# A graph and expert layer on one core: the first rows of x read and normalised ahead of the preparation of the edges

## What is computed

```python
edge_index = jnp.stack([src, dst])
xn = _layernorm(x, axis=-1)
x = x + _L0_gnn_ref(xn, edge_index, ...) + _L0_mix_ref(xn[None], w_qkv, w_proj, b_proj)[0]
x = x + _L0_ffn_ref(_layernorm(x, axis=-1)[None], ...)[0]
```

## Time and profile before

| | us |
|---|---|
| median of 3 runs | 1607.23 |
| lowest and highest | 1606.2, 1609.92 |
| the profiled execution | 1605.74 |
| its span in the trace | 1603.9 |
| mean granted clock of PE | 0.989 |

### The profile page before, as it was taken

One profiled execution on the slowest core, in us unless ns is written; L12 is line 12 of the kernel. 1 busy time (PEld: TensorE's weight loads), 2 busy tenths in 40 slices (PEclk: granted clock), 3 DMA queues, 4 the chain that ended last, 5 costly groups with the idle time before them and its releaser, 6 DMA issues.

```text
span 1603.9 us, 22049 instructions
## 1 busy us (share of the span) xinstructions
PE 1536.1 (96%) x8432; PEld 1025.1 (64%) x8433; DVE 791.6 (49%) x1503; ACT 347.0 (22%) x525; POOL 369.9 (23%) x422
## 2 busy tenths in 40 slices
PE   5999999999999899999989999999999999999996
PEld 3566676568889899999886555444444444444442
DVE  8655557886668799876987143111111111111111
ACT  3321122112240445640671110100000100000000
POOL 1187855653300000000000047011111111111111
PEclk9999999999999999999899999999999999999998
DMA  9900010000034427114203248834538211613450
GB/s 259 362 2 2 2 62 1 1 1 1 1 81 118 120 56 210 37 20 106 59 1 103 105 113 178 281 117 154 208 103 283 91 49 49 216 45 120 147 202 21
DMA packets 85339, 163.81 MB, mean 102 GB/s; under 512 B 18874, under 2 KB 48816, under 8 KB 85001
## 3 DMA queue, kind: packets, MB, share of 16 engines
q1 hardware_dynamic: 66903, 119.07, 23.4%
q0 software_dynamic: 12096, 23.27, 6.3%
q10 hardware_dynamic: 6258, 20.40, 4.6%
HBM read 127.75 MB, written 37.56 MB: 103 GB/s over the span
## 4 chain that ended last, share of the span: by engine, by line
PE 83%; DVE 9%; issue 2%; DMA 2%; ACT 1%; SPq 0%; DVEq 0%; POOL 0%; ACTq 0%; POOLq 0%
PE bank L816 33%; PE bank L1651 7%; PE bank L1689 6%; PE bank L1553 5%; PE bank L1466 5%; PE bank L1610 5%; PE bank L1438 4%; PE bank L726 2%; DVE arena L2419 2%; PE bank L1491 2%; PE bank L736 2%; PE bank L754 2%; DVE arena L2388 2%; PE bank L1737 1%; PE bank L810 1%
## 5 line engine op out<-in xcount | busy, mean ns | idle before, releaser
L816 PE MATMUL bank<-arena 128*64 128x384 f32 x3312 | 541.3, 488 | 0.6 <-ACT arena L890 0.6
L816 PEld LDWEIGHTS bank<-arena 128*64 128x64 f32 x3312 | 237.4, 137 | 292.8 <-issue 292.0
L1178 DVE SCALAR_TENSOR_TENSOR arena<-bank,arena 64x384 f32<-64x384 f32 x88 | 50.3, 610 | 356.2 <-DMA arena<-out_dram,arena 209.0
L1689 PE MATMUL bank<-arena 125*125 125x198 f32 (+1 forms) x1200 | 192.4, 322 | 10.3 <-DVE arena L2388 10.1
L1689 PEld LDWEIGHTS bank<-arena 125*125 125x125 f32 x1200 | 186.3, 196 | 14.4 <-DVE arena L2388 14.2
L1651 PE MATMUL bank<-arena 128*125 128x192 f32 x960 | 163.5, 328 | 1.1 <-DVE arena L2341 1.1
L1651 PEld LDWEIGHTS bank<-arena 128*125 128x125 f32 x960 | 157.7, 189 | 1.4 <-DVE arena L2341 1.4
L1344 POOL TENSOR_SCALAR arena<-arena 128x125 bf16<-128x125 f16 x186 | 115.3, 622 | 111.4 <-PE bank L1491 107.0
L2228 DVE TENSOR_TENSOR arena<-arena,bank 125x417 f32 x186 | 109.8, 590 | 52.4 <-PE bank L1491 43.3
L1338 POOL DMA_INDIRECT slot_table<-arena x80 | 112.0, 1400 | 93.4 <-issue 93.4
L707 POOL DMA_INDIRECT out_dram<-arena x44 | 40.1, 912 | 296.1 <-DVE arena L1178 296.1
(11 more groups left out here) (307 smaller groups left out, 1591.7 us busy)
## 6 DMA issues: line engine op xcount, KB each, us to landing
arena<-in_L_ffn_w_gate_dram SPq DMA_DIRECT2D x9, 2304.0 KB, 9.1
arena<-in_L_ffn_w_up_dram SPq DMA_DIRECT2D x9, 2304.0 KB, 10.8
arena<-in_L_ffn_w_down_dram SPq DMA_DIRECT2D x9, 2304.0 KB, 9.2
arena<-score_rows ACTq DMA_DIRECT2D x18, 585.9 KB
expert_in<-arena SPq DMA_DIRECT2D x23, 384.0 KB, 10.5
arena<-expert_in ACTq DMA_DIRECT2D x23, 384.0 KB, 3.5
arena<-in_L_mix_w_qkv_dram SPq DMA_DIRECT2D x2, 2304.0 KB, 17.6
xn_columns<-arena SPq DMA_DIRECT2D x1, 3750.0 KB, 14.8
```

The source lines that it names most:

```text
L816: ins = tp.matmul(ps[bank][HP * h:HP * h + HP, 0:384], frm[:, b, k, HP * h:HP * h + HP], ew[h][i][:, k, n * 384:(n + 1) * 384], start=(k = ...
L1689: ins = tp.matmul(ps[bank][0:T, c * width:(c + 1) * width], ptile[0:T, j % NPT, dt * T:(dt + 1) * T], values(n - first, st), start=(st == ...
```

## The change

Instructions are moved, one is added and one table load goes away. On SP, the two DMAs of rows 0 are issued ahead of the two DMAs of the edges. On DVE, the preparation of the edges is cut into `edges_as_float` (one cast) and `edge_places` (eleven instructions); the statistics of rows 0 come first, then the cast, then `normalise_rows(0)`, then the places. The one-hots and the key features are dealt out anew behind that. On PE, the transpose of the columns is now `turn_columns`, behind `turn_x(0)` and `turn_x(1)`. On ACT, a square root of one constant column is written to a scratch element as soon as the constants are ready, and the copy of the columns is now `take_columns`, behind `take_x(1)`.

```diff
--- before.py
+++ after.py
@@ -1208,8 +1208,6 @@
 
         @block.sync
         def _(sp):
-            sp.dma_start(ei[0:T, 0:EC], src.rearrange("(p c) -> p c", p=T)).then_inc(s_edges, 16)
-            sp.dma_start(ei[0:T, EC:2 * EC], dst.rearrange("(p c) -> p c", p=T)).then_inc(s_edges, 16)
             def rows_in(g):
                 rows_dma(sp, xs[0:T, 2 * g:2 * g + 2], x_rows[:, 2 * g:2 * g + 2], s_x[g])
 
@@ -1218,6 +1216,8 @@
                              w_qkv[:, D + hf * 384:D + (hf + 1) * 384].rearrange("(k p) n -> p k n", p=P)).then_inc(done, 16)
 
             rows_in(0)
+            sp.dma_start(ei[0:T, 0:EC], src.rearrange("(p c) -> p c", p=T)).then_inc(s_edges, 16)
+            sp.dma_start(ei[0:T, EC:2 * EC], dst.rearrange("(p c) -> p c", p=T)).then_inc(s_edges, 16)
             key_weights(0, s_wb[0])
             rows_in(1)
             key_weights(1, s_wk1)
@@ -1353,8 +1353,11 @@
         def _(pe):
 
             pe.wait_ge(s_const, 9)
-            pe.wait_ge(s_cin, 96)
-            tp.transpose(ps[7][:, 0:38], rowsin[0:38, :], ident[0:38, 0:38]).then_inc(s_colps, 1)
+
+            def turn_columns():
+                pe.wait_ge(s_cin, 96)
+                tp.transpose(ps[7][:, 0:38], rowsin[0:38, :], ident[0:38, 0:38]).then_inc(s_colps, 1)
+
             def turn_x(t):
 
                 pe.wait_ge(s_xn, t + 1)
@@ -1441,6 +1444,7 @@
 
             turn_x(0)
             turn_x(1)
+            turn_columns()
             key_product(0, 0)
             key_product(1, 0)
             turn_x(2)
@@ -1765,8 +1769,12 @@
             act.dma_start(rowsin[28:36, 0:C2], a_dst1.rearrange("h (f p) -> (h f) p", p=C2)).then_inc(s_cin, 16)
             act.dma_start(rowsin[36:38, 0:C2], b2.rearrange("(k p) -> k p", p=C2)).then_inc(s_cin, 16)
             act.wait_ge(s_const, 9)
-            act.wait_ge(s_colps, 1)
-            sc.activation(cols, ps[7][:, 0:38], ACT.Copy).then_inc(s_cols, 1)
+            sc.activation(junk8[0:T, 0:1], epst[0:T], ACT.Sqrt)
+
+            def take_columns():
+                act.wait_ge(s_colps, 1)
+                sc.activation(cols, ps[7][:, 0:38], ACT.Copy).then_inc(s_cols, 1)
+
             def ln_std(n):
                 lo, hi = LN_GROUPS[n]
                 act.wait_ge(s_stats, n + 1)
@@ -1790,6 +1798,7 @@
             ln_std(0)
             take_x(0)
             take_x(1)
+            take_columns()
             ln_std(1)
             key_exp(0, 0)
             key_exp(1, 0)
@@ -1977,29 +1986,32 @@
             stt = dv.scalar_tensor_tensor
 
 
-            dve.wait_ge(s_edges, 32)
-            step(dv.tensor_copy(ef[0:T], ei[0:T]))
...
-            dve.wait_ge(s_const, 9)
+            def edges_as_float():
+                dve.wait_ge(s_edges, 32)
+                step(dv.tensor_copy(ef[0:T], ei[0:T]))
+
+            def edge_places():
+                step.wait()
+                step(dv.tensor_scalar(pi[0:T], ef[0:T], 6554.0, None, ALU.mult))
+                step.wait()
...
+                dve.wait_ge(s_const, 9)
 
 
             def half(row, i):
@@ -2141,21 +2153,23 @@
                 stt(out=kbuf[t % 4][0:T, hf * 384:(hf + 1) * 384], in0=kexp[0:T, i % 2], scalar=1.0,
                     in1=krelu[0:T, i % 2], op0=ALU.min, op1=ALU.add).then_inc(s_kfeat, 1)
 
-            bucket_onehots(0)
             group_stats(0)
             ln_mean_var(0)
+            edges_as_float()
+            normalise_rows(0)
+            edge_places()
+            bucket_onehots(0)
+            group_stats(1)
+            ln_mean_var(1)
             bucket_onehots(1)
-            normalise_rows(0)
+            normalise_rows(1)
+            key_feature(0, 0)
             bucket_onehots(2)
             bucket_onehots(3)
-            group_stats(1)
-            ln_mean_var(1)
+            key_feature(1, 0)
             bucket_onehots(4)
-            normalise_rows(1)
-            key_feature(0, 0)
             edges_up_to(0)
             group_stats(2)
-            key_feature(1, 0)
             edges_up_to(1)
             group_stats(3)
             edges_up_to(2)
```

More of the change, by code:

```diff
@@ L1977, in _ @@
             stt = dv.scalar_tensor_tensor
-            dve.wait_ge(s_edges, 32)
-            step(dv.tensor_copy(ef[0:T], ei[0:T]))
[L1982 to L2001, removed]
-            dve.wait_ge(s_const, 9)
+            def edges_as_float():
[5 more added lines that the diff above has]
+                step.wait()
+                step(dv.tensor_scalar(ei[0:T], pi[0:T], 16, None, ALU.arith_shift_right))
+                step.wait()
+                step(dv.tensor_copy(pf[0:T], ei[0:T]))
+                step.wait()
+                step(stt(out=tf[0:T], in0=pf[0:T], scalar=-float(NT), in1=ef[0:T], op0=ALU.mult, op1=ALU.add))
+                step(dv.tensor_scalar(vh[0:T, 0], pf[0:T, 0:EC], 1.0, None, ALU.add))
+                step.wait()
+                step(stt(out=nd[0:T], in0=tf[0:T, EC:2 * EC], scalar=float(T), in1=pf[0:T, EC:2 * EC], op0=ALU.mult, op1=ALU.add))
+                step.wait()
+                step(dv.tensor_scalar(dgf[0:T], nd[0:T], float(G), None, ALU.is_ge))
+                step.wait()
+                step(stt(out=dgf[0:T], in0=nd[0:T], scalar=float(2 * G), in1=dgf[0:T], op0=ALU.is_ge, op1=ALU.add))
+                step.wait()
+                step(stt(out=nd[0:T], in0=dgf[0:T], scalar=-float(G), in1=nd[0:T], op0=ALU.mult, op1=ALU.add))
+                step(stt(out=dgf[0:T], in0=tf[0:T, 0:EC], scalar=float(DG), in1=dgf[0:T], op0=ALU.mult, op1=ALU.add))
+                step.wait()
+                step(dv.tensor_scalar(vh[0:T, 1], nd[0:T], 1.0, None, ALU.add))
+                dve.wait_ge(s_const, 9)
```

## The result

| | before | changed |
|---|---|---|
| median of 22 runs, us | 1606.37 | 1608.87 |
| lowest and highest | 1599.92, 1609.92 | 1602.76, 1613.92 |
| profiled execution | 1605.74 | 1611.96 |
| its span | 1603.9 | 1610.1 |

The changed kernel is slower: the ratio is 1.0021, with a 95% interval from 1.0011 to 1.003. Of 1606 us that is 3.4 us (1.8 to 4.8); the two medians differ by 2.5. The forecast was +1.6 us, a median of 1608.8 where 1608.87 was measured. That the two medians agree is luck, since the forecast started from the 1607.23 known then and not from the 1606.37 of all runs. So the way is right, the size is half of the measured one, and the ratio is just beyond the 0.2% within which it was expected.

The account below looks back on a forecast made before the run. DVE's unbroken work up to the third running sum was taken to bound the start, PE the rest. Counts -0.6 us and clock loss +2.2 us on the 1607.23 known gave a median of 1608.8, range 1604.8 to 1611.8.

Parts of the forecast that it names:

- The frame: First 50 us: when DVE ends the third running sum matters, not how much sooner PE starts.
- The rival of the head start: At the counts: DVE was not what PE waited for, so 5.4 us reach the end, 1601.8; chance 0.05.
- Parts 1 and 2, the landings: Start to counts: rows 0 land at 6.2, weights 12.8, rows 1 16.1; PE gets its counts at 38.9, -0.6 us.
- The same bytes stand ahead of it: First half of the key weights: issued at 2.37 behind unchanged bytes, so landing at 12.8, just in time.
- Part 3, the clock: Behind the counts: PE's 6.7 us wait drops the clock to 0.50, slowing two key products, +2.2 us.
- The sum: Whole kernel: -0.6 for the counts and +2.2 for the clock, giving a median of 1608.8 us.

Follow-up runs that it names:

- e4: Kernel before with DVE's first key feature moved behind the first running sum; ratio 0.9987 (0.9975 to 1.0).
- e6: Changed kernel with key_product(1, 1) moved ahead of the counts and key_product(2, 1) ahead of edge_starts; ratio 1.0006 (0.9993 to 1.002).
- e9: Kernel before with the edits of e4, e10 and e5, and the last one-hots ahead of the second statistics; 1603.45 against 1606.59, ratio 0.9976 (0.9965 to 0.9987).
- e3: Changed kernel with 14 extra matmuls, read by nobody, on PE ahead of the counts; ratio 1.0016 (1.0003 to 1.0029) against the kernel before.
- e7: Changed kernel with 9 extra matmuls, read by nobody, on PE ahead of the counts; ratio 1.0003 (0.9989 to 1.0016) against the kernel before.
- e10: Kernel before with GpSimd's memset of the running sums' mask moved behind DVE's first one-hots; ratio 0.999 (0.9977 to 1.0003).
- e1: Changed kernel with SP's old order, both edge DMAs ahead of rows 0; ratio 1.0026 (1.0014 to 1.0039) against the kernel before.
- e5: Kernel before with only the change's ACT and PE part: early root, columns turned and copied behind the second tile; ratio 1.0009 (0.9997 to 1.0021).
- e2: Kernel before with rows 0 requested ahead of the edges on SP, DVE's order unchanged; ratio 1.0019 (1.0004 to 1.0033).

## Why the prediction was right, and where it was wrong

**The frame was right.** "The question is not how much sooner PE starts, but how much sooner DVE ends the third running sum, and what PE does in the meantime": e4, e6 and e9 show the first half, e3 and e7 the second. The rival of the head start is out. PE did start 4.3 us sooner, and all of it was spent waiting or in slower passes. That it waited 6.68 us where 6.7 were forecast is luck: its products ended at 35.5 and not at 32.2, the counts came as much later, and in the second profile the wait was 8.29.

**Parts 1 and 2, the landings: the term was mis-sized, and its sign was wrong.** -0.6 us was forecast for the counts; it is +2.7 against the first profile, +2.8 to +3.2 from the changed kernel's two to the other two. The intervals between events were right: from the rows to PE 3.6 us forecast and 3.6 measured (7.34 to 10.98), from the second key feature to the counts 15.6 and 15.7 (26.42 to 42.16). The landings were not. Rows 0 came at 7.34 instead of 6.2; the weights at 14.65 instead of 12.8, and their first 24 passes took 10.7 us; rows 1 at 18.38 instead of 16.1. How long these 24 passes take differs from one execution to the next: 8.9 in the second profile of the changed kernel, 9.3, 8.8 and 8.9 in the three of the kernel before. There the two later ones have the counts 0.4 to 0.6 us sooner than the first, by a shorter wait of DVE for the first key feature. Both arms met at the second key feature, as said, but at 26.4, not at 23.3; in the second profile DVE did not wait there at all. The error is in how were read. A count of large packets tells when so many bytes have been moved, and that is not the moment at which the waiting engine goes on. The changed kernel's own trace has it, from 0 to 6.5 and from 7 to 7.5 us:

```profile
DMA packets 356, 0.98 MB, mean 151 GB/s; under 512 B 46, under 2 KB 231, under 8 KB 356
...
DMA packets 139, 0.14 MB, mean 287 GB/s; under 512 B 12, under 2 KB 139, under 8 KB 139
```

By 6.5 us 356 - 231 = 125 large packets have flown, all of rows 0; the count was full at 6.0 already, and from there to 7.5 not one more flew. DVE gets the rows at 7.34, 1.3 us later. What fills the 1.3 us was not looked into. For rows 1 the reading was also out for the kernel before: e10 shows them at 17.2 with the edges first, where 16.1 was read. With the rows first they land at 17.9 to 18.7 in five profiles (e3, e7, the changed kernel twice, e6), so the change itself seems to cost them about 1 us more; on the other side stands e10 alone, since in the other profiles with the edges first they are there when DVE asks, at 17.7 to 18.4. The weights are later as well: 12.8 to 14.0 in eight profiles with the edges first, 13.7 to 14.7 in six with the rows first. "The same bytes stand ahead of it" was true and did not fix the time.

**What was not counted.** DVE's start. Before, its unbroken work began with the edges at 4.8; now with the rows at 7.3. I looked at whether rows 1 would be late, not at the 2.5 us that DVE gives away at its very start. They are not lost whole: the second instruction no longer meets the memset (0.32 us at 11.34 instead of 1.51), which the prediction said makes no difference, and which softened the loss.

**Part 3, the clock: right in kind and near in size, but not net.** Forecast: 0.50 for 3 to 5 us, two key products in 10.4 us, 2.2 us lost. Measured: 5.4 us behind the counts, 6.74 + 4.14 = 10.9 us, 2.6 lost. What I did not know is that the kernel before mostly pays as well: in two of its three profiles its 2.1 us wait costs 5.82 - 4.12 = 1.7 us. Net of that the change costs 0.9 us of clock there. The claim that "after the 2.1 us wait the granted clock stayed at 1.00" was true of one execution. The Trainium skill's page "TensorE: Matmul & The Clock Gate" ("What's actually happening") warns that the number of slow matmuls at the start of a kernel differs from run to run. The profiles here agree for the start, with 8.8 to 9.3 us for the same 24 passes, and show the same behind a wait, with 2.08 us of it and 4.12 or 5.82 us for the twelve passes.

**The sum.** +1.6 was -0.6 for the counts and +2.2 for the clock. It is about +3 and +0.9, together 3.7 to 4.2 at the first rank product against the usual execution of before, and 3.4 in the runs. The two errors have opposite signs, about +3.6 in the counts and -1.3 in the clock; that the total missed by only 1.8 us is luck, and the order of the two causes was wrong.

**Not settled.** Why the transfers behind rows 0 land about 1 us later when rows 0 go first was not taken apart. Nor was what sets the length of the low level. It is 3.4 us in all where the wait was 2.08 or 3.27 us (five profiles). Behind 6.67 and 6.68 us (e1 and the changed kernel) it is 6.8 in all, of which 4.6 and 5.4 lie behind the counts, and behind 8.29 it is 10.2, of which 5.4 lie behind them.

## What to carry to other kernels

Before an engine is started sooner, find the first point at which it waits for another, and ask when that other one starts: here DVE, with 35 us of work and hardly a gap, was the bound, and taking 2 us of its idle away (e4) was worth what 4.3 us of head start on PE were not. A landing is read from the instruction that waits for it or from the issue's own time to landing, not from counts of packets; the landings read here missed by 1.1 to 2.3 us, so where nothing waits, give them 1 to 2 us of doubt. And a single profile shows one side of the clock's coin: look at a second one before pricing a wait of 2 us.

## What the runs showed of the hardware

- At the counts, a wait of PE of 2.08 us let the granted clock fall in four profiles (e5, e10 and two of the kernel before) and not in two (e2, the first of the kernel before); waits of 0.26 to 1.73 never did, of 3.27 to 8.29 always. The fall can come late: behind a wait of 2.08 us it came 1.0 to 1.5 us after PE was back at work, behind 3.27 us 0.5 after; behind 6.67 to 8.29 it came within the wait.
- Matmuls that fill a wait can pay: with 18 passes whose result nobody reads, the twelve passes behind took 4.11 us instead of 6.74, and the ratio was 1.0003 (0.9989 to 1.0016) instead of 1.0021 (1.0011 to 1.003).
- Two small transfers of 78 KB each, issued behind 750 KB, landed at 9.27 instead of 4.3 to 5.0 us, and the 750 KB at 7.1 to 7.8 instead of 9.74.
- An instruction of DVE on 320 elements took 1.51 us beside a memset of GpSimd and 0.33 without it (e10). Not every instruction suffers: in e10 the memset (10.15 to 11.58) stands beside the statistics of rows 0, and these take 1.93 us as elsewhere. The Trainium skill's page "SBUF — State Buffer" ("SBUF: two separate sides") has a pair of ports that GpSimd shares with VectorE instructions in a two-port mode, among others; the first to start locks it, and the other is blocked for the whole of that instruction. The first profile agrees in that the 1.51 us (5.34 to 6.85) ended 0.2 us behind the memset (5.18 to 6.67). No run tells a lock from another cause, or in which mode that instruction ran.
